# Expert 1 as two exact runs of steps (43 tokens, 496 columns), and twelve warming products on TensorE

## What is computed

```python
def step(h, xt):
    m = concatenate([xt, h]) @ weight + bias
    c = tanh(m[:, units:]); g = sigmoid(m[:, :units] + 1.0)
    return g * h + (1.0 - g) * c
x = x + scan(step)                       # 64 steps in a row
# L_head = L_wrist = 64 // 3 = 21, the rest (proprio) has 22 steps
w_be = top-2 of softmax(gate), normalised          # one weight per batch and expert
mask[1, 21:42] = 0                                 # expert 1 gives nothing to the wrist steps
mask[2, :21] = 0                                   # expert 2 gives nothing to the head steps
for e in range(4):
    out += w_be[:, e] * mask[e] * (gelu(x @ ew1[e] + eb1[e]) @ ew2[e] + eb2[e])
out += gelu(x @ sw1 + sb1) @ sw2 + sb2             # 256 -> 1024 -> 256
x = x + out
```

## Time and profile before

| | |
|---|---|
| three runs | 640.73, 640.94, 641.15 us |
| profiled execution, its own time | 641.29 us |
| its span, first to last instruction | 639.5 us |
| TensorE matmul busy | 628.3 us, 98% |
| VectorE busy | 407.4 us, 64% |
| ScalarE busy | 314.5 us, 49% |
| GpSimd busy | 253.3 us, 40% |
| DMA | 20.81 MB, mean 33 GB/s |

### The profile page before, as it was taken

One profiled execution on the slowest core, in us unless ns is written; L12 is line 12 of the kernel. 1 busy time (PEld: TensorE's weight loads), 2 busy tenths in 40 slices (PEclk: granted clock), 3 DMA queues, 4 the chain that ended last, 5 costly groups with the idle time before them and its releaser, 6 DMA issues.

```text
span 639.5 us, 16406 instructions
## 1 busy us (share of the span) xinstructions
PE 628.3 (98%) x5704; PEld 536.4 (84%) x5704; DVE 407.4 (64%) x953; ACT 314.5 (49%) x599; POOL 253.3 (40%) x501
## 2 busy tenths in 40 slices
PE   9999999999999999999999999999999999999995
PEld 6999888888888888888788888888898888888894
DVE  5998987566565665667777645544556675554464
ACT  5655554334443334434646544444456664444452
POOL 1657776445554455434335430232033431343000
PEclk9999999999999999999999999999999999999998
DMA  6520210000000000000001200000001220000006
GB/s 254 195 82 24 66 53 2 0 1 1 0 0 0 0 0 0 0 2 2 0 1 60 74 0 0 0 0 0 0 1 51 84 84 0 0 0 0 0 2 263
DMA packets 8026, 20.81 MB, mean 33 GB/s; under 512 B 816, under 2 KB 1584, under 8 KB 7472
## 3 DMA queue, kind: packets, MB, share of 16 engines
q1 hardware_dynamic: 7696, 19.63, 8.9%
q10 hardware_dynamic: 288, 0.64, 0.3%
HBM read 16.08 MB, written 4.19 MB: 32 GB/s over the span
## 4 chain that ended last, share of the span: by engine, by line
PE 95%; DVE 3%; issue 1%; ACT 0%; POOL 0%; ACTq 0%; DVEq 0%; POOLq 0%
PE zy L1052 57%; PE hp L1052 38%; DVE w_buf L677 0%; DVE d_t L697 0%; DVE h_b L700 0%; DVE acc L998 0%; DVE d_t L694 0%; DVE h_b L684 0%; DVE first L704 0%; ACT y_all L654 0%; DVE g_lo L671 0%; DVE h_r L685 0%; DVE shared_buf L743 0%; DVE h_b L688 0%; DVE x_hl L746 0%
## 5 line engine op out<-in xcount | busy, mean ns | idle before, releaser
L671 DVE TENSOR_TENSOR g_lo<-g_f,g_hi 128x512 fp32r<-128x512 f32 (+3 forms) x167 | 119.4, 716 | 151.5 <-ACT g_hi L536 147.6
L1052 PE MATMUL zy<-g_hi,w_buf 128*128 128x512 f32 (+3 forms) x704 | 180.7, 378 | 0.3 <-issue 0.3
L536 ACT ACTIVATE g_hi<-g_f 128x512 fp32r<-128x512 f32 (+3 forms) x176 | 106.4, 604 | 148.5 <-PE zy L1052 148.2
L529 ACT ACTIVATE g_f<-hp,first 128x512 f32<-128x512 f32 (+4 forms) x180 | 118.9, 661 | 116.3 <-PE hp L1052 110.2
L1052 PE MATMUL hp<-shared_buf,w_buf 128*128 (+1 forms) x672 | 165.3, 381 | 0.0
L1052 PEld LDWEIGHTS zy<-g_hi,w_buf 128*128 128x128 f32 x704 | 125.1, 188 | 22.3 <-ACT g_hi L536 0.5
L1052 PEld LDWEIGHTS hp<-shared_buf,w_buf 128*128 128x128 f32 x672 | 124.3, 188 | 23.1 <-issue 0.3
L1052 PE MATMUL hp<-x_hl,w_buf 128*128 (+2 forms) x432 | 104.7, 378 | 0.2 <-DVE w_buf L677 0.2
L1052 PE MATMUL zy<-g_lo,w_buf 128*128 128x512 f32 (+3 forms) x352 | 103.8, 376 | 0.0
L1052 PEld LDWEIGHTS zy<-h_b,y_all 128*128 128x128 bf16 x2976 | 90.7, 98 | 15.5 <-issue 13.1
L1052 PE MATMUL zy<-h_b,y_all 128*128 128x64 bf16 x2976 | 98.4, 193 | 0.8 <-DVE h_b L700 0.6
(11 more groups left out here) (153 smaller groups left out, 488.2 us busy)
## 6 DMA issues: line engine op xcount, KB each, us to landing
stage<-in_w_exp SPq DMA_DIRECT2D x40, 256.0 KB, 2.8
out_y<-acc SPq DMA_DIRECT2D x2, 1376.0 KB, 5.3
acc<-in_x SPq DMA_DIRECT2D x1, 2048.0 KB, 9.0
acc<-in_x SPq DMA_DIRECT2D x1, 1536.0 KB, 9.2
out_y<-acc SPq DMA_DIRECT2D x1, 1344.0 KB, 5.1
acc<-in_w SPq DMA_DIRECT2D x1, 512.0 KB, 4.6
acc<-in_x SPq DMA_DIRECT2D x2, 256.0 KB, 6.2
acc<-in_w ACTq DMA_DIRECT2D x1, 512.0 KB, 5.5
```

The lines of the kernel that those rows point to most:

```text
L529: act.activation(raw_of(j, n, keep), hp[j % 2][:, 0:n], ACT.Gelu_apprx_tanh, bias=par[:, S_B1 + e * NCH + j:S_B1 + e * NCH + j + 1]).then_ ...
L536: act.activation(chunk_of(j, n, keep)[0], raw_of(j, n, keep), ACT.Copy).then_inc(ghi_done, 1)
L671: dve.tensor_tensor(lo, raw_of(j, n, keep), hi.bitcast(F32), ALU.subtract).then_inc(glo_done, 1)
L1052: return pe.matmul(out_, lhsT=lhsT, rhs=rhs, start=start, stop=stop, skip_group_check=True)
```

## The change

Expert 1 takes 43 tokens of a batch: steps 0 to 20 and steps 42 to 63. The runs have different lengths (21 and 22), so that one access pattern no longer covers both, and each slot is gathered with two copies and added with two additions. The half slot keeps its 22 tokens. A group has 43 x 11 + 22 = 495 used columns (`USED`), and the instructions of TensorE and ScalarE and `split_lo` take 496 (`COLS`). Step 21 remains only in the first half of a split batch; the multiplication by 0 now covers one token of each half of the features instead of twelve. The experts with one run lose an axis of length 1 in their patterns. The warming products go from sixteen to twelve, and the third count of `opened` comes with the twelfth.

```diff
-RUNS = [(0, 1, T, T), (0, 2, 2 * HEAD, PROP), (HEAD, 1, T, T - HEAD), (0, 1, T, T)]
-TOKS = [n * length for _, n, _, length in RUNS]
+RUNS = [[(0, T)], [(0, HEAD), (PROP_AT, PROP)], [(HEAD, T - HEAD)], [(0, T)]]
+TOKS = [sum(length for _, length in runs) for runs in RUNS]
...
-COLS = [TOKS[e] * p - (PROP if q == SPLIT else 0) for q, (e, p) in enumerate(zip(RUN_OF, PER))]
+COLS = [TOKS[e] * p - (TOKS[e] - PROP if q == SPLIT else 0) for q, (e, p) in enumerate(zip(RUN_OF, PER))]
+USED = COLS[SPLIT]
+COLS[SPLIT] = USED + USED % 2
...
+        def runs_of(e):
+            at = [sum(length for _, length in RUNS[e][:i]) for i in range(len(RUNS[e]))]
+            return [(run, slice(a, a + run[1])) for run, a in zip(RUNS[e], at)]
...
-                        last = pool.tensor_copy(dst.rearrange("p i s k (a n) -> p (i s k) a n", a=RUNS[e][1]),
-                                                tokens_of(x_hl, e, bs[s]))
+                        for run, c in runs_of(e):
+                            last = pool.tensor_copy(dst[:, :, c], tokens_of(x_hl, run, bs[s]))
...
-                    keep = con[:, C_MASK:C_END][:, bass.ds((r - sv[q]) % 2, WIDE)]
-                    dve.tensor_tensor(masked_steps(y_w), masked_steps(y_w), keep.unsqueeze(1).to_broadcast([P, K, WIDE]),
-                                      ALU.mult).then_inc(y_read, 1)
+                    keep = con[:, C_MASK:C_END][:, bass.ds((r - sv[q]) % 2, 1)]
+                    tail = y_w[:, :, per * n + HEAD:USED]
+                    dve.tensor_tensor(tail, tail, keep.unsqueeze(1).to_broadcast([P, K, 1]), ALU.mult).then_inc(y_read, 1)
...
-                        dst = tokens_of(acc, e, b)
-                        src = src.rearrange("p k (a n) -> p k a n", a=RUNS[e][1])
-                    dve.tensor_tensor(dst, dst, src, ALU.add).then_inc(add_done, 1 if s < PER[q] - 1 else WIDE - s)
+                        for run, c in runs_of(e):
+                            dst = tokens_of(acc, run, b)
+                            last = dve.tensor_tensor(dst, dst, src[:, :, c], ALU.add)
+                    last.then_inc(add_done, 1 if s < PER[q] - 1 else WIDE - s)
...
-            for i, bank in enumerate([hp[0], hp[1], zy[:, 4], zy[:, 5], zy[:, 0], zy[:, 1]] + [zy[:, 2], zy[:, 3]] * 5):
+            for i, bank in enumerate([hp[0], hp[1], zy[:, 4], zy[:, 5], zy[:, 0], zy[:, 1]] + [zy[:, 2], zy[:, 3]] * 3):
                 last = mm(bank[:, 0:512], none[:, 0:P], none[:, 0:512], True, True)
-                if i in (1, 5, 15):
+                if i in (1, 5, 11):
                     last.then_inc(opened, 1)
```

More of the change, by code:

```diff
@@ L43 @@
 ORDER = [E, 0, 3, 1, 2]
-RUNS = [(0, 1, T, T), (0, 2, 2 * HEAD, PROP), (HEAD, 1, T, T - HEAD), (0, 1, T, T)]
-TOKS = [n * length for _, n, _, length in RUNS]
-MASKED_EXPERT, MASKED_STEP = 1, HEAD
 PROP_AT = 2 * HEAD
+RUNS = [[(0, T)], [(0, HEAD), (PROP_AT, PROP)], [(HEAD, T - HEAD)], [(0, T)]]
+TOKS = [sum(length for _, length in runs) for runs in RUNS]
+MASKED_EXPERT = 1
 assert PROP == HEAD + 1
@@ L114 @@
 C_MASK = C_CUT + len(CUT_AT)
-C_END = C_MASK + WIDE + 1
+C_END = C_MASK + 2
 S_B1, S_B2, S_GW, S_TW, S_GB, S_TB, S_B0 = 0, 40, 50, 74, 90, 94, 102
@@ L307, in pieces_at, with flat @@
             return [[], [0], [1], [2], [3], [4], [5], [6, 7]][j]
[L309 to L321, removed]
+        def flat(v):
             if len(v.shape) == 5:
@@ L324, in half_of, with tokens_of @@
             return v.rearrange("p k t b -> p k (t b)")
+        def tokens_of(t, run, b):
+            first, length = run
+            return flat(t[..., first:first + length, bass.ds(b, 1)])
+        def half_of(t, par, b):
+            return flat(t[..., bass.ds(par * PROP_AT, PROP), bass.ds(b, 1)])
+        def runs_of(e):
+            at = [sum(length for _, length in RUNS[e][:i]) for i in range(len(RUNS[e]))]
+            return [(run, slice(a, a + run[1])) for run, a in zip(RUNS[e], at)]
         def slot_cols(q, s):
             n = TOKS[RUN_OF[q]]
[L329 to L334, removed]
+            return slice(s * n, USED if q == SPLIT and s == WIDE - 1 else (s + 1) * n)
         block = ctx.enter_context(nc.Block())
@@ L466, in gather @@
                 for s in range(PER[q]):
-                    dst = xg[:, bass.ds(r % 2, 1), :, :, slot_cols(q, s)]
+                    dst = xg[:, bass.ds(r % 2, 1), :, :, slot_cols(q, s)].rearrange("p i s k n -> p (i s k) n")
                     if q == SPLIT and s == WIDE - 1:
-                        last = pool.tensor_copy(dst.rearrange("p i s k n -> p (i s k) n"),
-                                                half_of(x_hl, (r - sv[q]) % 2, bs[s]))
-                    else:
-                        last = pool.tensor_copy(dst.rearrange("p i s k (a n) -> p (i s k) a n", a=RUNS[e][1]),
-                                                tokens_of(x_hl, e, bs[s]))
+                        last = pool.tensor_copy(dst, half_of(x_hl, (r - sv[q]) % 2, bs[s]))
+                    else:
+                        for run, c in runs_of(e):
+                            last = pool.tensor_copy(dst[:, :, c], tokens_of(x_hl, run, bs[s]))
                 last.then_inc(gather_done, 1)
@@ L880, in gather_first @@
                     for s in range(at, upto):
-                        dst = xg[:, 0, :, :, s * n:(s + 1) * n].rearrange("p s k (a n) -> p (s k) a n", a=RUNS[RUN_OF[0]][1])
-                        last = dve.tensor_copy(dst, tokens_of(x_hl, RUN_OF[0], bs[s]))
+                        dst = xg[:, 0, :, :, s * n:(s + 1) * n].rearrange("p s k n -> p (s k) n")
+                        last = dve.tensor_copy(dst, tokens_of(x_hl, RUNS[RUN_OF[0]][0], bs[s]))
                     if upto == SLOTS:
@@ L934, in weigh @@
                             last = dve.scalar_tensor_tensor(
-                                out=y_w[:, k, per * n:COLS[q]], in0=y_bank(r)[k][:, per * n:COLS[q]], scalar=b2,
-                                in1=slot_w[:, bass.ds(r * WIDE + per, 1)].to_broadcast([P, COLS[q] - per * n]),
+                                out=y_w[:, k, per * n:USED], in0=y_bank(r)[k][:, per * n:USED], scalar=b2,
+                                in1=slot_w[:, bass.ds(r * WIDE + per, 1)].to_broadcast([P, USED - per * n]),
                                 op0=ALU.add, op1=ALU.mult)
@@ L968, in add_slots @@
                         dst = half_of(acc, (group - sv[q]) % 2, b)
+                        last = dve.tensor_tensor(dst, dst, src, ALU.add)
                     else:
-                        dst = tokens_of(acc, e, b)
-                        src = src.rearrange("p k (a n) -> p k a n", a=RUNS[e][1])
-                    dve.tensor_tensor(dst, dst, src, ALU.add).then_inc(add_done, 1 if s < PER[q] - 1 else WIDE - s)
+                        for run, c in runs_of(e):
+                            dst = tokens_of(acc, run, b)
+                            last = dve.tensor_tensor(dst, dst, src[:, :, c], ALU.add)
+                    last.then_inc(add_done, 1 if s < PER[q] - 1 else WIDE - s)
             def slots_at(q, per, i):
@@ L995, in finish_last @@
                             order_add((r + 1 + k) * WIDE + 1, s)
-                        dst = tokens_of(acc[:, k:k + 1], e, bs[s])
-                        src = y_w[:, k:k + 1, s * n:(s + 1) * n].rearrange("p k (a n) -> p k a n", a=RUNS[e][1])
+                        dst = tokens_of(acc[:, k:k + 1], RUNS[e][0], bs[s])
+                        src = y_w[:, k:k + 1, s * n:(s + 1) * n]
                         dve.tensor_tensor(dst, dst, src, ALU.add).then_inc(add_done, 1 if s < LAST - 1 else WIDE - s)
@@ L1381 @@
     consts[:, C_CUT:C_CUT + len(CUT_AT)] = CUT_AT
-    consts[:, C_MASK + WIDE] = 1.0
+    consts[:, C_MASK + 1] = 1.0
     consts[:, C_TIE:C_TIE + E * E] = (routed[None, :] < routed[:, None]).ravel()
```

## The result

The changed kernel takes 637.5 us (median of 4 runs, 637.39 to 637.89) where the kernel before takes 640.91; ratio 0.9946, interval 0.9934 to 0.9957. The forecast was 637.6 in a range of 636.6 to 639.6. The total came out right, and in part by luck: the warming products brought less than forecast and the additions cost more, 0.7 us together, and a gain of 0.8 us that nobody forecast made up for both. The two profiled executions (641.29 and 637.89 us; spans 639.54 and 636.11) show it, read in the order of the program.

What follows compares the result with a forecast made beforehand. TensorE, without idle time in expert 1's stage, was taken as the bound. From 641.29, less 3.2 and 0.85, plus 0.75, gave 638.0 for the profiled execution; the median forecast was 637.6 us, range 636.6 to 639.6.

Steps and rivals of the forecast that it cites:

- Term 1: Expert 1's 480 products go from 506 to 496 columns on TensorE: 6.7 ns less each, 3.2 us gained.
- The rule of 16 columns: A TensorE product was held to take 32 ticks plus its columns rounded up to a multiple of 16; 528 ticks at 496.
- The second rival: Expert 1's columns bring less: pace falls by 4.2 to 4.4 ns a product, 2.0 us in all, total 638.8; chance 0.09.
- its other form: Products of 496 columns stay at 226.7 ns, so the columns bring nothing: 640.8 us; chance 0.06.
- Term 2: At the start, four warming products removed at the full clock: 0.85 us gained, bounds 0.2 and 0.85.
- the fourth rival: At the start, TensorE's clock does not rise and stays at 1.2 GHz through the first steps; 645.6 us if until 17 us; chance 0.05.
- Term 3: Doubled additions for expert 1's fifth group make VectorE later in expert 2's group: 0.75 us lost, bounds 0 and 2.4.
- the other four groups: Expert 1's groups added while TensorE works at its own pace; twice the additions stay under a 2.72 us chunk, costed at nothing.
- the gather: GpSimd's doubled copies for expert 1: 11 more, 3.7 us, covered by 14.2 us of idle time, costed at nothing.
- No loss on VectorE: In expert 2's group the ordering wait hides all second additions: 636.9 us; chance 0.13.
- VectorE as the bound: VectorE bounds the last group, through waited additions and register loads: 639.2 us, or 641.4 at full cost; chance 0.07.
- The clock: TensorE's clock not rising after fewer warming products: the 32 products from 7.24 us take about 3.6 us more; chance 0.05.

## Why the prediction was right or wrong

**Term 1, fewer columns.** Right in size: 6.7 ns and 3.2 us forecast, 219.9 ns a product and 3.23 us in the trace, 3.15 us by the kernel with 506 columns. Its ground was partly wrong. The rule of 16 columns fitted the three widths that the prediction read, and 502 columns break it; a step of 8 would have fitted them too and gives the same for 496. What carried the number was the neighbourhood: 506 at the pace of 512, and 496 close to the line between 430 and 512. That line was worked out wrongly: 193.3 + 66 x 33.4/82 is 220.2 ns and so 6.5 less, not 219.8 and 6.8. The second rival, a line of 4.2 ns, is refuted at 496 (3.2 us and not 2.0), and so is its other form. The Trainium skill's gap formula (the section named above) fits the bf16 products and not these.

**Term 2, the warming products.** 0.85 us was the upper bound and not the likely value. The traces give 0.6 (changed kernel), 0.7 (means of `hp<-acc`) and the runs 0.5 (twelve products alone) to 0.9. The step that failed is the one that took the rise at 6.4 us for fixed. It moves from one execution to the next, from 3.9 to 6.9 us in twelve traces; when it is early the seeds bound the start, when it is late the first products of the first step run at 1.2 GHz. The Trainium skill's sentence (TensorE: Matmul & The Clock Gate, What's actually happening) that the window runs freely was quoted beside the fourth rival and was given no weight in the forecast; the traces agree with it, by the times just named.

**Term 3, the additions.** The mechanism and its place were right, its size was not: 0.75 us forecast, 1.16 measured (1.19 with nothing else changed), inside the bounds. Six additions span 1.06 us where three took 0.82, from the first start to the last 0.82 instead of 0.48, so 0.11 us a slot and not 0.08. The estimate of the lateness lacked what stands between a split and its first addition, the load of three numbers: it starts when the last addition has been issued, so VectorE's sequencer, and not its arithmetic, sets the period. Neither the load nor the second addition makes the wait by itself: without the additions of steps 0 to 20, or with the numbers loaded elsewhere, TensorE waits for nothing there. Costing the other four groups at nothing was right: TensorE is busy for all of the 107 us from 500 to 607. So was the gather: 22 copies take 7.65 us for 5.76, and GpSimd still stands idle for 12.3 us after them.

**Not in the prediction.** 0.77 us at the end, most likely from where the code of VectorE falls. In the profiled executions it turned a forecast that would have been 0.7 us too low, by terms 2 and 3, into one that is 0.1 too high.

**Rivals.** No loss on VectorE: refuted by both kernels with doubled additions. VectorE as the bound: true in kind, at half the price given. The clock: not with twelve products, but with eight, at the price worked out.

## What to carry to other kernels

When an engine that is far from busy (VectorE, 65%) holds many small instructions with addresses from registers, count its issue time and its register loads in the stage where the main engine waits soonest; here 0.24 us for each loaded number mattered as much as the doubled additions, and moving the loads took the whole wait away with every addition kept. Loads of such numbers belong under long instructions or in an earlier stage with slack, in pieces. The pace of fp32r products should be measured at the width wanted, and in the kernel itself: rounding up to 8 columns fits the kernels here and fails for the same products by themselves.

## What the runs showed of the hardware

- fp32r products of 506 and 512 columns have one pace (226.7 ns), 502 have 223.3 and 496 have 220.0 in the kernel; in these kernels the pace is 32 ticks of 2.4 GHz and the columns rounded up to 8. By themselves the products do not follow it, and 432 columns are slower than 430 (196.2 and 193.4 ns).
- The clock of TensorE rises at another time in each execution: its first record stands between 3.9 and 6.9 us in twelve traces, and with the same sixteen products before it the first step began between 6.57 and 7.53 us. Whether twelve make the times steadier is open: the 11 runs of the kernel before with twelve lie within 0.33 us, against 1.5 us in 27 runs with sixteen, but the 11 runs of the 506-column kernel, with twelve too, spread over 1.33 us.
- In 13 traces the end of the program takes 6.0 us where two transfers of code (queue q14) fall into it and 5.2 to 5.5 us where one does, and shifting VectorE's code led from one case to the other. That is of the size of the edits studied here. A comparison of two kernels at 0.1% includes it.
